# Gathers paced by picks, and long scans, in a graph network of seven passes

## The reference

```
messages = x[src] * edge_probs[:, None] * weight          # L0
m = einsum('ei,eio->eo', hx[edge_src], W)                 # L1, twice
out = segment_sum(h[src] * alpha[:, :, None], dst)        # L2, twice
s = segment_sum(x[src] * mask[:, None], dst)              # L3, twice
```

## Time and profile before

| what | value |
|---|---|
| median of 3 runs | 36,993.97 us (36,990.56 to 37,006.73) |
| the profiled execution's own time | 37,013.04 us |
| its span, first to last instruction | 37,011.7 us |
| busy share of TensorE, VectorE, GpSimd; ScalarE | 54%, 49%, 43%; 8% |
| granted TensorE clock, mean share of full speed | 0.731 |

### The profile page before, as it was taken

One profiled execution on the slowest core, in us unless ns is written; L12 is line 12 of the kernel. 1 busy time (PEld: TensorE's weight loads), 2 busy tenths in 40 slices (PEclk: granted clock), 3 DMA queues, 4 the chain that ended last, 5 costly groups with the idle time before them and its releaser, 6 DMA issues.

```text
span 37011.7 us, 276253 instructions
## 1 busy us (share of the span) xinstructions
PE 19835.6 (54%) x89726; PEld 9384.5 (25%) x89726; DVE 18318.8 (49%) x38447; ACT 2910.9 (8%) x6609; POOL 16095.0 (43%) x16846
## 2 busy tenths in 40 slices
PE   3455545555545555544444466666555555666665
PEld 1122222222222222222222222222222223222222
DVE  4455555555545555535555544444444443444443
ACT  2333300000000000000000000000000000000000
POOL 4444444444444444444444444444344444343434
PEclk7777767777767777767777677777677776777777
DMA  3222211111111111112222122222222221111111
GB/s 97 73 84 86 85 46 51 51 52 51 46 44 50 52 52 51 48 45 76 76 76 77 52 60 63 62 61 63 58 77 75 76 77 57 46 44 46 45 45 39
DMA packets 1271680, 2237.21 MB, mean 60 GB/s; under 512 B 386665, under 2 KB 737274, under 8 KB 1261818
## 3 DMA queue, kind: packets, MB, share of 16 engines
q1 hardware_dynamic: 729380, 2025.85, 16.6%
q0 software_dynamic: 538944, 192.26, 5.3%
q10 hardware_dynamic: 1942, 1.43, 0.0%
HBM read 1597.46 MB, written 620.66 MB: 60 GB/s over the span
## 4 chain that ended last, share of the span: by engine, by line
another core or an unknown queue 32%; DVE 26%; PE 21%; issue 14%; DVEq 6%; ACT 1%; DMA 0%; POOL 0%; ACTq 0%; SPq 0%; POOLq 0%
PE psB L764 17%; DVE Sb L1280 5%; DVE xT L1160 4%; DVE prod L1321 4%; DVE sub L1166 2%; DVEq L1165 2%; DVE xT L1156 2%; PE psB L835 2%; DVEq L1189 1%; DVE arena L1127 1%; PE psB L901 1%; DVE arena L1190 1%; PE psA L795 1%; DVE prod L1324 1%
## 5 line engine op out<-in xcount | busy, mean ns | idle before, releaser
L764 PE MATMUL psB<-xp,arena 128*128 128x476 bf16 x26040 | 6967.2, 421 | 5890.9 <-DVE xT L1160 3205.7
L764 PE MATMUL psB<-ext,arena 128*128 128x308 bf16 (+1 forms) x17388 | 3599.5, 357 | 2903.7 <-issue 2291.2
L764 PEld LDWEIGHTS psB<-xp,arena 128*128 128x128 bf16 x26040 | 2625.3, 108 | 9904.3 <-issue 7375.5
L1156 DVE TENSOR_TENSOR xT<-psB,XT 128x616 bf16<-128x616 f32 (+1 forms) x1860 | 1803.3, 978 | 4564.0 <-remote 3526.7
L1160 DVE TENSOR_TENSOR xT<-psB,sub 128x476 bf16<-128x476 f32 x2976 | 1916.5, 645 | 4114.7 <-remote 3498.9
L528 POOL DMA_INDIRECT gb<-tab3b,typi x2356 | 2228.8, 946 | 3325.3 <-DVE prod L1411 2485.0
L528 POOL DMA_INDIRECT gb<-tab1b,srci x2356 | 2289.1, 972 | 3100.6 <-DVE prod L1326 2291.5
L528 POOL DMA_INDIRECT gb<-tab1a,srci x2356 | 2291.7, 973 | 3026.5 <-DVE prod L1326 2274.4
L528 POOL DMA_INDIRECT gb<-tab2b,srci x2356 | 2223.2, 944 | 2616.9 <-DVE prod L1387 1917.2
L835 PE MATMUL psB<-w2as,hid 64*128 64x256 f32 x12896 | 2166.5, 454 | 2048.8 <-issue 1201.3
L1321 DVE TENSOR_TENSOR prod<-psB,gb 128x1024 f32<-128x1024 f32 x1612 | 1974.3, 1225 | 2579.8 <-remote 2051.4
(11 more groups left out here) (337 smaller groups left out, 19398.2 us busy)
## 6 DMA issues: line engine op xcount, KB each, us to landing
arena<-oh_d SPq DMA_DIRECT2D x1861, 448.0 KB
hid<-oh_d SPq DMA_DIRECT2D x639, 448.0 KB
oh_d<-arena SPq DMA_DIRECT2D x558, 448.0 KB
ext<-oh_d SPq DMA_DIRECT2D x290, 448.0 KB
S2a<-Sb SPq DMA_DIRECT2D x62, 1404.0 KB
S2b<-Sb SPq DMA_DIRECT2D x62, 884.0 KB
ext<-in_attrT SPq DMA_DIRECT2D x404, 128.0 KB
S3a<-Sb SPq DMA_DIRECT2D x62, 832.0 KB
```

The lines of the kernel that those rows point to most:

```text
L764: m = pe.matmul(psB[b][:, o:o + W], pk.onehot(n)[:, g, u * P:(u + 1) * P], pk.part(g, q).bitcast(BF16), start=g == 0, stop=g == NB - 1)
L1156: v.tensor_tensor(to.rearrange("p (b f x) -> p b f x", b=2, x=2 * JB), psB[b][:, :].rearrange("p (b w) -> p b w", b=2)[:, :, 0:W].rearrang ...
```

## The change

Two things are changed together.

1. In every pass, from the third chunk on, GpSimd waits before every fifth gather i of a chunk until VectorE has kept i * OFF / (TC - OFF) - 2 (rounded down) picked columns of that same chunk; where that number is not positive there is no wait.
2. In passes 1, 2 and 5 the messages are written feature by feature, each feature as 52 values behind one carry value, into two halves of the tile Sb. ScalarE spreads same over a decay tile of the same shape (`repeat_same`), whose carry places stay 0. VectorE copies the last values of the chunk before into the carry places (`carry`) and runs one scan over all 16 x 53 elements in passes 1 and 2, or four over 8 x 53 in pass 5 (`long_sums`). ScalarE copies the result into the order of Sd[k] (`store_part`) and issues the store itself; SP no longer does. Before the fix-up of the pass's ends VectorE copies the last state out (`finish`).

```
@@
+TW = TC + 1
+LONG = (1, 2, 5)
+LEAD = 2
@@
+        def tall(c, f):
+            o = (c % 2) * f * TW
+            return v3(Sb[:, o:o + f * TW], TW)
+        def tall_rows(c, f, lo, hi):
+            o = (c % 2) * f * TW
+            return Sb[:, o + lo * TW:o + hi * TW]
+        def store_tile(k, c):
+            n = TC * fwidth[k]
+            o = 2 * 32 * TW + (c % 2 * n if k < 5 else 0)
+            return v3(Sb[:, o:o + n], fwidth[k])
+        def decay_tile(k, c):
+            n = fwidth[k] * TW
+            if k == 5:
+                return prod[:, 0:n]
+            o = TC * 16 + (c % 2) * TC * 36
+            return gb[:, o:o + n]
@@ sync_program, stream
-                    put(k, c)
+                    if k not in LONG:
+                        put(k, c)
@@ gpsimd_program, gathers
                     for i in range(TC - OFF[k]):
+                        kept = i * OFF[k] // (TC - OFF[k]) - LEAD
+                        if c >= 2 and i % 5 == 0 and kept > 0:
+                            pool.wait_ge(d_keep, PICK[k].call0 + c * OFF[k] + kept)
@@ scalar_program
+            def repeat_same(k, c):
+                if c == 0:
+                    a.wait_ge(d_ready, LONG.index(k) + 1)
+                back = 1 if k == 5 else 2
+                if c >= back:
+                    a.wait_ge(d_sum, NCH * k + c - back + 1)
+                a.activation(v3(decay_tile(k, c), TW)[:, :, 1:TW], bc(same[:, span(c)], 1, fwidth[k]), ACT.Copy).then_inc(a_decay, 1)
+            def store_part(k, c, i, n):
+                f = fwidth[k]
+                lo, hi = f * i // n, f * (i + 1) // n
+                if i == 0:
+                    a.wait_ge(d_sum, NCH * k + c + 1)
+                    e = c - 1 if k == 5 else c - 2
+                    if e >= 0:
+                        a.wait_ge(l_out[e % 2], 16 * (31 * k + e // 2 + 1))
+                m = a.activation(store_tile(k, c)[:, :, lo:hi], tall(c, f)[:, lo:hi, 1:TW].rearrange("p f t -> p t f"), ACT.Copy)
+                if i == n - 1:
+                    m.then_inc(a_put, 1)
+                    a.wait_ge(a_put, longs(k, c) + 1)
+                    a.dma_start(rows(Sd[k], f)[:, span(c), :], store_tile(k, c)).then_inc(l_out[c % 2], 16)
@@ hidden_units (passes 1 and 2)
+                k = 1 + rep
+                repeat_same(k, 0)
                 for h in range(NH):
+                    c, i = divmod(2 * h - 3, TC // 4)
+                    if c and i // 2 == 1:
+                        store_part(k, c - 1, 0, 1)
+                    if c >= 0 and i // 2 == 4 and c + 1 < NCH:
+                        repeat_same(k, c + 1)
@@ first_rows (pass 5)
+                    c, i = divmod(n + 1, pk.pairs)
+                    if i == 0 and 2 <= c <= NCH:
+                        repeat_same(5, c - 1)
+                    c, i = divmod(n, pk.pairs)
+                    if c >= 2 and i < 2:
+                        store_part(5, c - 2, i, 2)
@@ vector_program
+            def carry(k, c):
+                f = fwidth[k]
+                if c >= 2:
+                    v.wait_ge(a_put, longs(k, c) - 1)
+                if c:
+                    v.drain()
+                    v.tensor_copy(tall(c, f)[:, :, 0], tall(c + 1, f)[:, :, TC])
+            def long_sums(k, c, done, parts):
+                pk, f = PICK[k], fwidth[k]
+                share = pk.share(c, done)
+                v.wait_ge(a_decay, longs(k, c) + 1)
+                v.drain()
+                for i in range(parts):
+                    if i:
+                        done = picks(k, done, pk.until(c, share + (0.9 - share) * i / parts), f)
+                    lo, hi = f * i // parts, f * (i + 1) // parts
+                    at = tall_rows(c, f, lo, hi)
+                    m = v.tensor_tensor_scan(at, decay_tile(k, c)[:, lo * TW:hi * TW], at, 0.0, ALU.mult, ALU.add)
+                m.then_inc(d_sum, 1)
+                return done
@@ net_pass (passes 1 and 2)
-                msg = v3(prod[:, 2048:2048 + TC * 16], 16)
+                    msg = tall(c, 16)[:, :, 1:TW].rearrange("p f t -> p t f")
                     arrived(k, c)
+                    carry(k, c)
-                    done = sums(k, c, 16, done, range(16), lambda q: msg[:, :, q], lambda q: same[:, span(c)])
+                    done = long_sums(k, c, done, 1)
@@ typed_pass (pass 5)
+                        carry(k, c)
+                        v.drain()
+                        v.tensor_tensor(tall(c, width)[:, :, 1:TW].rearrange("p f t -> p t f"), got(c, width),
+                                        bc(wE[:, span(c)], 2, width), ALU.mult).then_inc(d_gbfree, 1)
+                        done = long_sums(k, c, done, 4)
```

More of the change, by code:

```diff
@@ L260, in gnn_program @@
             sem(f"t_{n}") for n in ("pick", "turn", "typed", "hidden", "weight", "fix", "turned", "made", "mid", "head"))
-        a_hid, a_row, a_exp, a_fixexp, a_turned, a_gate, a_done, a_code, a_got = (
-            sem(f"a_{n}") for n in ("hid", "row", "exp", "fixexp", "turned", "gate", "done", "code", "got"))
+        a_hid, a_row, a_exp, a_fixexp, a_turned, a_gate, a_done, a_code, a_got, a_decay, a_put = (
+            sem(f"a_{n}") for n in ("hid", "row", "exp", "fixexp", "turned", "gate", "done", "code", "got", "decay", "put"))
+        d_ready, d_last = (sem(f"d_{n}") for n in ("ready", "last"))
         ident = cst[:, CI:CI + P]
@@ L326, in state, with longs @@
             return v3(Sb[:, o:o + TC * f], f)
+        def tall(c, f):
[14 more added lines that the diff above has]
+            return gb[:, o:o + n]
+        def longs(k, c):
+            return NCH * LONG.index(k) + c
         def last_state(k):
+            if k in LONG:
+                return Sb[:, TC * 32 * 3 + 128:TC * 32 * 3 + 128 + fwidth[k]]
             return state(NCH - 1, fwidth[k])[:, TC - 1, :]
@@ L856, in fix_sums @@
                 f = fwidth[k]
-                pe.wait_ge(d_sum, NCH * (k + 1))
+                if k in LONG:
+                    pe.wait_ge(d_last, LONG.index(k) + 1)
+                else:
+                    pe.wait_ge(d_sum, NCH * (k + 1))
                 pe.transpose(psA[0][0:f, 0:P], last_state(k), ident).then_inc(t_fix, 1)
@@ L1282, in sums, with begin, finish @@
                 return done
+            def begin(k):
+                v.drain()
+                v.memset(tall(0, fwidth[k])[:, :, 0], 0.0)
+                if k == 5:
+                    for i in range(2):
+                        v.wait_ge(l_tab3[i], 16 * 14)
+                for i in range(1 if k == 5 else 2):
+                    m = v.memset(decay_tile(k, i), 0.0)
+                m.then_inc(d_ready, 1)
+            def carry(k, c):
[18 more added lines that the diff above has]
+                return done
+            def finish(k):
+                v.drain()
+                v.tensor_copy(last_state(k), tall(NCH - 1, fwidth[k])[:, :, TC]).then_inc(d_last, 1)
             def lists_to_psum():
@@ L1404, in typed_pass @@
                 pr = v3(prod[:, 0:TC * width], width)
+                if k in LONG:
+                    begin(k)
                 done = picks(k, 0, pk.until(-1, 1), width)
@@ L1409, in typed_pass @@
                         v.wait_ge(a_got, (c + 1) * pk.pairs)
[L1410 to L1413, removed]
+                    if k in LONG:
+                        carry(k, c)
+                        v.drain()
+                        v.tensor_tensor(tall(c, width)[:, :, 1:TW].rearrange("p f t -> p t f"), got(c, width),
+                                        bc(wE[:, span(c)], 2, width), ALU.mult).then_inc(d_gbfree, 1)
+                        done = long_sums(k, c, done, 4)
+                    else:
+                        v.drain()
+                        v.tensor_tensor(pr, got(c, width), bc(wE[:, span(c)], 2, width), ALU.mult).then_inc(d_gbfree, 1)
+                        v.drain()
+                        done = sums(k, c, width, done, range(width), lambda q: pr[:, :, q], lambda q: same[:, span(c)])
                     done = picks(k, done, pk.until(c, 1), width)
+                if k in LONG:
+                    finish(k)
                 if k == 5:
```

7 lines of the change are left out of this document (added).

## The result

| | kernel before | with the change |
|---|---|---|
| median, us | 37,000.35 (36,990.56 to 37,007.97, 4 runs) | 30,712.74 (30,632.27 to 30,796.1, 4 runs) |
| profiled execution, us | 37,013 | 30,765.29 (span 30,764.0) |
| mean granted clock | 0.731 | 0.794 |

The ratio is 0.8302, 95% interval 0.8286 to 0.8318. The prediction was 30,200 with 24,800 to 36,400.

A forecast was written before the change was run, and what follows sets the result against it. No engine is full; TensorE's stall during long gather runs costs about half of each chunk. 62 x (321.9 floor + 126 stalls) = 27,770, plus 350 start-up and 2,257 outside, less 161 scans: 30,216, called 30,200 us; range 24,800 to 36,400.

The forecast's parts named there:

- the stall: TensorE issues only every 1.4 us, from some 14 us into a run of gathers to about 6 us after it.
- Short runs do no harm: Node stage after pass 3: a run of 14 supposed gathers, 18 us, then 12 us rest, does no visible harm.
- Two of 9 us a chunk: Leading case, chance 0.42: with paced gathers two stalls remain, 18 us a chunk, 126 over the seven passes.
- the tank: Stall model: 11 gathers in 14 us fill it, 6 us rest empties it; outflow 0.56 a us, content 3.4.
- The floor: Chunk time without the stall, the larger of VectorE's and GpSimd's time: 321.9 us together over the seven passes.
- The scans: Long scans save 1.3 us a chunk in passes 1 and 2, 161 us in all; pass 5 counted as 0.
- no change: A long scan may hold one gather once a chunk, as the fifteen scans already did; bounds 0 and 2 us.
- lateness at nothing: VectorE waiting at the next chunk's start for delayed gathers costs nothing; with cover gone, 3.75 us a chunk.
- the ordering copy: New ScalarE copy in passes 1, 2 and 5, hidden in idle time: 0.84 us for 832 elements.
- Start-up: The first two chunks of each pass go unpaced, some 50 us over the floor each pass, 350 us.
- the stall all but goes: Rival, chance 0.22: pacing nearly removes the stall, 22,404 us, up to 27,000 with one stall a chunk.
- the loss follows the count of gathers: Rival, chance 0.24: 0.94 us lost a gather however spread; only the scans help, 36,700 us, or 33,000 and up.
- each cut makes a stall of its own: Rival, chance 0.12: each wait before a fifth gather adds a stall; at 6.5 us a cut, 38,900 us.

The follow-up runs named there:

- e9_change_again: The changed kernel itself, word for word, run again on quiet chip C: 22,269.0 us, ratio 1.0013 to the kernel before.
- e1_pace_only: The kernel before with the waits before every fifth gather and nothing else, on quiet chip A: 22,267.69 us, ratio 1.0017.
- v1_unpaced: The changed kernel without waits, long scans in passes 1 and 2 only, two more picks and two fewer gathers in pass 4, on stalling chip D: 37,192.04 us.
- v2_paced: v1_unpaced with the waits before every fifth gather added, on stalling chip D: 30,755.15 us, ratio 0.833 to the kernel before.

## Why the prediction was right, and where it wasn't

**What bounds the kernel.** Right for the chip that the trace came from, and most of the reading of the stall held: TensorE alone is slow, the DMA engines aren't (the gathers' queue took 6.5% of 16 engines in 30,764 us and 8.7% in 22,259, so 2,000 and 1,937 us; the other large queue 5,845 and 5,876), and the clock is a result (the first slow window has 0.72 in the earlier trace rows and 0.79 in the changed kernel, later ones 0.50). "Short runs do no harm" rested on a misreading: the 14 DMAs of the earlier trace rows are scatters. What the prediction didn't see, and one trace can't show, is that the stall isn't the kernel's alone: three chips of four run the same program without it.

**The stalls.** Two of 9 us a chunk, 126 us over the passes, was the term that decided. Measured, by two executions of one program: 122.9. The sum was closer than its parts, and that is luck: the tank gave 18 us in each pass, and measured it is 14 to 17 in passes 0, 1, 2, 4 and 5, 20.6 in pass 3 and 23.4 in pass 6. Counted in the trace, VectorE stands for more than 4 us 1.2 to 2.4 times a chunk, 7 to 17 us each; in pass 6 the pieces are few and long (1.2 of 17 us), not two of 9. (Not all of that standing is the stall: in e9_change_again VectorE stands so for 3.6, 5.9 and 7.5 us a chunk in passes 0, 4 and 5.)

How a stall depends on the run of gathers before it can be counted in the changed kernel's stalling trace. Let a run end where GpSimd stands for more than 1.5 us, and ask in how many runs a stand of VectorE of over 4 us begins, up to 2 us behind the run's end:

| gathers in the run | runs | with a stand |
|---|---|---|
| 1 to 5 | 118 | 2 |
| 6 to 10 | 352 | 117 |
| 11 to 15 | 238 | 160 |
| 16 to 20 | 214 | 210 |
| over 20 | 174 | 173 |

So gathers in runs of up to five do next to no harm, and eleven isn't a sharp edge. The lengths weren't set by an experiment, though, and a stall itself ends a run at GpSimd's next wait. That fits something that fills up and empties, but the tank's two figures (0.56 gathers a us out, 3.4 held) weren't tested: the runs meant for it, with finer and coarser waits and with half the gathers, fell on quiet chips.

**The floor.** 319.3 us with the scans taken off, measured 328.5: 570 us too little over 62 chunks, the largest miss, and the term that was mis-sized. By pass, predicted and measured: 40 and 44.1; 48.4 and 50.1, twice; 45 and 44.9; 47.5 and 47.2; 42.5 and 45.0; 47.5 and 47.1. Pass 0 lacks 4.1 us because I counted its 32 gathers alone, and GpSimd has 2,180 instructions there for 1,984 gathers: 3.2 more a chunk, of 1.25 us each. The earlier trace rows already had 2,144 of them. In passes 1 and 2 the chunk was 1.3 us longer than VectorE's busy time over 0.95 to begin with (51.0 without gathers, against 49.7), and the scans gave 0.4 less than forecast.

**The scans.** Their own cost was right (by form, VectorE, changed kernel):

```profile
L1388 DVE TENSOR_TENSOR_SCAN Sb<-prod,Sb 128x424 f32<-128x424 f32 x248 | 256.8, 1037 | 6.0 <-issue 0.4
...
L1388 DVE TENSOR_TENSOR_SCAN Sb<-gb,Sb 128x848 f32<-128x848 f32 x124 | 238.7, 1925 | 11.9 <-issue 0.9
```

1.93 and 1.04 us against 2.0 and 1.07 expected: 2.09 ns an element. The Trainium skill, "DVE: opcode table, instruction layouts, handler registers and perf-mode slots", section "Datapath and trigger behaviour", says that the scan runs at half throughput; with the 0.96 GHz of "VectorE: DVE Perf Modes", section "Specifications", that is an estimate of 2.08 ns an element, and the trace agrees. The gain was over-sized: 0.9 us a chunk in passes 1 and 2, not 1.3, and in pass 5 a loss of 1.6 on a quiet chip instead of nothing. There GpSimd is the bound, and its gathers take 1,031 ns on average in e9_change_again, against 984 in e1_pace_only. The timeline of e9_change_again shows how, in pass 1:

```profile
4023.34 1.93 DVE L1388 TENSOR_TENSOR_SCAN Sb<-gb,Sb 128x848 f32<-128x848 f32 x1
...
4023.52 2.50 POOL L561 DMA_INDIRECT gb<-tab1a,srci  x1 [0.83 <-DVE Sb L1440]
...
4025.30 1.78 ACT L667 ACTIVATE Sb<-Sb 128x832 f32<-128x832 f32 x1 [5.94 <-DVE Sb L1388]
```

A gather that starts beside the scan takes 2.50 us instead of 0.94 and ends 0.75 us after the scan does. I had this as "no change" for one scan a chunk; with four scans a chunk in pass 5, 383 gathers of e9_change_again run beside one and take 1.40 us on average, the other 1,725 take 0.95, and against the short scans it is 47 ns x 34 gathers = 1.6 us, all of the loss. The Trainium skill, "SBUF — State Buffer", section "SBUF: two separate sides", says that a VectorE instruction with two inputs in SBUF holds the port pair that it shares with GpSimd for its whole length; this row agrees with it, if issuing a gather reads SBUF.

**Lateness and ScalarE.** On a quiet chip lateness at nothing held within 0.1 us a chunk except in pass 0 (0.7). Of ScalarE's copies the decay copy was right (0.89 us for 832 elements, 1.58 for 1,664), and the ordering copy was under-sized: 832 elements take 1.78 us, where I had 0.84. Both are hidden; ScalarE now works 6.8 us a chunk in passes 1 and 2 and 10.0 in pass 5, far from full.

**The rest of the sum.** Start-up was put at 350 us and is 551 (28,538 of the passes less 62 x 451.4). Outside the passes 2,226 against 2,257. Against the profiled execution: floor and scans +570, stalls -192, start-up +201, outside -31, together +548 on 30,216, which gives 30,764. The errors partly cancel, so the total, 1.8% off, is closer than its terms.

**The rivals.** That the stall all but goes is excluded by the windows around 15,042; that the loss follows the count of gathers by v1_unpaced and v2_paced, which issue equally many and differ by 6,437 us; that each cut makes a stall of its own by the same pair.

**What stays open.** Why some chips stall and others don't, and what TensorE waits for, was not settled. The traces speak against one candidate, that TensorE waits for its own instructions to be loaded: the DMA queue that I take to bring them (q8, kind "instruction") has 744 packets in each trace, with a median of 1,016 ns in the changed kernel's stalling trace and 1,021 in its quiet one, and TensorE's slow steps lie at all distances behind such a packet. Whether it belongs to the chip or to something around it at that time isn't shown either. Chip A was quiet in two sets of runs an hour apart, the second seven minutes after chip D stalled; but on chip C, otherwise quiet, one of the 15 executions of the kernel before took 25,428 us at a clock of 0.786, and no trace of it was kept. A direct DMA, a finer pace or gathers of fewer rows on a stalling chip were not measured.

## What to carry to other kernels

An engine that is slowed with "issue" as its only reason, while all others have their usual durations, may be slowed by where the program runs: run the kernel before on more than one chip before explaining its idle time. Where long runs of indirect DMAs stall TensorE, break them up with waits on the consumer's own progress; here that is worth 17% where the stall exists and costs 0.2% where it doesn't. Before calling a run of DMAs in a trace evidence on gathers, look at its operands: they say whether it gathers or scatters. When a floor is made from an engine's instruction time, count all instructions of the window, not those of the main loop, and look at what a longer instruction of the neighbour does to each of them.

## What was not expected of the hardware

- The kernel before takes 22,209 to 22,239 us on three chips and 36,936 to 37,000 in the two sets of runs that stalled; the changed kernel's VectorE, GpSimd and ScalarE have the same busy times within 0.5% in both places.
- Where the kernel stalls, a run of 99 indirect DMAs turns 58 us of mixed work into 140, and a run of up to five gathers is followed by a stand of VectorE in 2 of 118 cases, one of 16 to 20 in 210 of 214.
- A gather of 128 rows holds GpSimd for 944 ns with 300 more to the next, a direct DMA into the same tile 540.
- ScalarE's copy with a strided read (832 elements, read feature by feature, written edge by edge) takes 1,781 ns; the decay copy of as many elements, which reads and writes in one order, takes 888.
